# The neighbours' first layer as four column tiles, and a fp32 second layer with zero-padded weights

## The reference

```python
h = maximum(layernorm(x), 0)                          # 4096 x 256
neib_att = tanh(neigh @ Wn1 + bn1) @ Wn2 + bn2        # 4096x256 @ 256x32, then @ 32x32
value    = neigh @ Wv + bv                            # 4096 x 128
x_att    = tanh(h @ Wx1 + bx1) @ Wx2 + bx2            # 4096 x 32
ws  = leaky_relu(x_att @ neib_att.T, 0.01)            # 4096 x 4096
ws  = softmax(where(adj > 0, ws, -9e15), axis=1)
out = x + concatenate([h @ Wfx + bfx, ws @ value], axis=1)
```

## Time and profile before

| | us |
|---|---|
| median of 3 runs (519.1 to 520.16) | 519.95 |
| the profiled execution | 519.84 |
| its span, first to last instruction | 518.0 |

### The profile page before, as it was taken

One profiled execution on the slowest core, in us unless ns is written; L12 is line 12 of the kernel. 1 busy time (PEld: TensorE's weight loads), 2 busy tenths in 40 slices (PEclk: granted clock), 3 DMA queues, 4 the chain that ended last, 5 costly groups with the idle time before them and its releaser, 6 DMA issues.

```text
span 518.0 us, 8865 instructions
## 1 busy us (share of the span) xinstructions
PE 480.9 (93%) x2812; PEld 374.6 (72%) x2855; DVE 451.8 (87%) x883; ACT 417.6 (81%) x585; POOL 210.0 (41%) x324
## 2 busy tenths in 40 slices
PE   5697978799999999999999999999999999998996
PEld 4365667587778778777878777877777787766884
DVE  1679878989999899989998999899999989985664
ACT  2562797899889988998889888988899889997552
POOL 1503113145644564446544664366336444530100
PEclk9997998999999999999999999999999999999999
DMA  6864774565456544664567445744565555500100
GB/s 180 217 203 79 142 137 79 113 112 94 81 92 139 116 76 85 127 144 81 82 127 156 77 75 105 159 80 80 110 135 82 82 95 118 90 5 1 42 0 22
DMA packets 38530, 52.07 MB, mean 101 GB/s; under 512 B 4436, under 2 KB 30292, under 8 KB 38484
## 3 DMA queue, kind: packets, MB, share of 16 engines
q0 software_dynamic: 9216, 33.56, 39.3%
q1 hardware_dynamic: 29268, 17.95, 11.7%
HBM read 80.86 MB, written 4.19 MB: 164 GB/s over the span
## 4 chain that ended last, share of the span: by engine, by line
PE 55%; ACT 17%; issue 9%; POOL 7%; DVE 7%; DMA 4%; SPq 1%; DVEq 0%; ACTq 0%; POOLq 0%
PE ps_turned L904 14%; PE ps_scores L881 9%; ACT scores L515 7%; PE ps_product L925 7%; PE ps_product L923 7%; PE ps_product L924 6%; POOL scores L409 5%; ACT scores L503 5%; ACT pt_hi L479 4%; PE ps_scores L880 4%; PE ps_product L849 3%; DMA scores<-in_L_gnn_neigh 3%; DVE mask L645 2%; DVE pt_lo L658 1%; PE ps_product L787 1%
## 5 line engine op out<-in xcount | busy, mean ns | idle before, releaser
L658 DVE TENSOR_TENSOR pt_lo<-ps_turned,pt_hi 128x512 fp32r<-128x512 f32 x256 | 173.4, 684 | 34.3 <-ACT pt_hi L479 19.1
L479 ACT ACTIVATE pt_hi<-ps_turned 128x512 fp32r<-128x512 f32 x256 | 155.4, 608 | 56.5 <-PE ps_turned L904 56.2
L409 POOL TENSOR_TENSOR scores<-scores,mask 128x512 f32<-128x512 f32 x109 | 126.7, 1162 | 176.7 <-ACT scores L503 176.6
L904 PE MATMUL ps_turned<-ident,scores 128*128 128x128 f32 x1024 | 154.7, 274 | 3.6 <-DVE pt_lo L658 3.1
L904 PEld LDWEIGHTS ps_turned<-ident,scores 128*128 128x128 f32 x1024 | 124.1, 140 | 45.5 <-DVE pt_lo L658 17.2
L503 ACT ACTIVATE scores<-ps_scores 128x1024 f32<-128x1024 f32 x128 | 132.0, 1031 | 13.3 <-PE ps_scores L881 13.3
L515 ACT ACTIVATE scores<-scores,neg_top 128x2048 f32<-128x2048 f32 x64 | 129.0, 2015 | 0.0
L676 DVE CUSTOM_DVE_ANT_0 scores<-ps_scores,scores,top 128x1024 f32<-128x1024 f32 x96 | 122.5, 1276 | 3.2 <-ACT scores L503 2.7
L923 PE MATMUL ps_product<-pt_hi,v_hi 128*128 128x512 f32 x256 | 122.0, 477 | 0.2 <-DVE pt_lo L658 0.2
L881 PE MATMUL ps_scores<-neib,xs 128*128 128x512 f32 x256 | 109.9, 507 | 6.0 <-DVE top L676 2.9
L925 PE MATMUL ps_product<-pt_lo,v_hi 128*128 128x512 f32 x256 | 101.4, 396 | 0.0
(11 more groups left out here) (75 smaller groups left out, 378.1 us busy)
## 6 DMA issues: line engine op xcount, KB each, us to landing
adj_in<-in_adj POOLq DMA_DIRECT2D x64, 512.0 KB, 5.4
scores<-in_L_gnn_neigh SPq DMA_DIRECT2D x8, 512.0 KB, 5.5
x_rows<-in_x SPq DMA_DIRECT2D x8, 512.0 KB, 5.4
x_left<-in_x SPq DMA_DIRECT2D x8, 256.0 KB, 3.0
x_right<-in_x SPq DMA_DIRECT2D x8, 256.0 KB, 2.8
out_h<-x_left SPq DMA_DIRECT2D x8, 256.0 KB, 4.2
out_h<-x_right SPq DMA_DIRECT2D x8, 256.0 KB, 3.4
scores<-in_x SPq DMA_DIRECT2D x1, 512.0 KB, 4.0
```

The lines of the kernel that those rows point to most:

```text
L409: pool.tensor_tensor(half, half, mask[:, s % MASK_RING, BANK:CHUNK], ALU.add).then_inc(masked, 1)
L479: act.activation(pt_hi[:, (2 * b + u) % HI_RING], pt[:, u], ACT.Copy).then_inc(hi_done, 1)
L658: dve.tensor_tensor(pt_lo[:, u], pt[:, u], pt_hi[:, (2 * b + u) % HI_RING].bitcast(FP32), ALU.subtract).then_inc(lo_done, 1)
L904: last = pe.transpose(pt[:, u, i * P:(i + 1) * P], scores[:, parity * TILES + i, n * P:(n + 1) * P], ident[:, :])
```

## The change

The first layer of the neighbours takes the form of x's: `w1_n` is held once, 32 wide, and `first_layer` issues for each half of the contraction four matmuls of 128 neighbours each, each into its own 32 partitions of `ps_hidden`, now 128x128. Tanh is taken once in 128x128 (L444's line). The second layer is four fp32 matmuls of 128 columns, each with `w2_n[:, i, :]`, which is zero but in the 32 rows of strip i. So `hidden_stack`, `w2_stack`, the fp32r copy, the subtraction and the three DVE instructions that built `w2_stack` are gone, and with them the semaphores `hidden_hi`, `hidden_lo`, `w2_hi` and `w2_done`. `att_high` moves from DVE to ACT as an `Identity` activation with bias; in the loop it follows the tanh, for group 7 it stands in step 0. SP issues one DMA for `Wn1` where there were two, and four for `Wn2` where there was one, after a wait until POOL has zeroed `w2_n` and `w2_x`; PE and ACT still wait for all of these before turn 0 (`CONSTS_IN`).

```diff
--- before.py
+++ after.py
@@ -54,7 +54,7 @@
 DMA_RING = 512
-CONSTS_IN = 16 * 4, 16 * 6
+CONSTS_IN = 16 * 6, 16 * 6
 B2_IN = 16 * 2
@@ -140,21 +140,18 @@
         rows = scratch(4, 0, 2, TILES, D_IN)
-        hidden = scratch(4, 2048, 2, GROUP)
-        w1_n = scratch(4, 3072, KT, P)
-        w2_n = scratch(4, 3328, D_HID)
+        hidden = scratch(4, 2048, 2, P)
+        w1_n = scratch(4, 3072, KT, D_HID)
+        w2_n = scratch(4, 3328, TILES, P)
         x_ahead = scratch(5, 3072, TILES, D_IN)
         w_v = scratch(5, 0, KT, D_OUT)
-
-        hidden_stack = pt_hi[:, 0:2, :]
-        w2_stack = pt_lo[:, 0, 0:P]
 
...
         pa = ctx.enter_context(nc.psum_tensor("ps_product", [P, 2, BANK], FP32))
-        ps_hidden, ps_value = pa[:, 0, :], pt
+        ps_hidden, ps_value = pa[:, 0, 0:P], pt
         ps_att = [ps[:, 1, BANK:CHUNK], pa[:, 1, :]]
@@ -259,20 +254,19 @@
             load_neigh(0)
-            for k in range(KT):
-                sp.dma_start(w1_n[:, k].rearrange("p (r h) -> p r h", h=D_HID),
-                             wn1[k * P:(k + 1) * P, :].rearrange("p (r h) -> p r h", r=1).to_broadcast(
-                                 [P, P // D_HID, D_HID])).then_inc(consts_in[0], 16)
+            sp.dma_start(w1_n, wn1.rearrange("(k p) h -> p k h", p=P)).then_inc(consts_in[0], 16)
             sp.dma_start(b1[:, 0:1], bn1.rearrange("(r p a) -> r p a", r=1, a=1).to_broadcast(
...
             load_x_rows(0)
-            sp.dma_start(w2_n, wn2.rearrange("(r p) h -> r p h", r=1).to_broadcast(
-                [P // D_HID, D_HID, D_HID])).then_inc(consts_in[0], 16)
+            sp.wait_ge(cleared, 2)
+            for j in range(TILES):
+                sp.dma_start(w2_n[j * D_HID:(j + 1) * D_HID, j, :].rearrange("p (r h) -> p r h", h=D_HID),
+                             wn2.rearrange("p (a h) -> p a h", a=1).to_broadcast(
+                                 [D_HID, P // D_HID, D_HID])).then_inc(consts_in[0], 16)
             sp.dma_start(w1_x[:, :, :], wx1.rearrange("(k p) h -> p k h", p=P)).then_inc(consts_in[1], 16)
...
                 [P // D_HID, D_HID, 1])).then_inc(consts_in[1], 16)
-            sp.wait_ge(cleared, 1)
             for j in range(TILES):
@@ -336,6 +330,7 @@
 
+            pool.memset(w2_n, 0.0).then_inc(cleared, 1)
             pool.memset(w2_x[:, :, :], 0.0).then_inc(cleared, 1)
@@ -426,6 +421,13 @@
         def _(act):
+            def att_high(par, q):
+                if q == 0:
+                    act.wait_ge(b2_in, B2_IN)
+                act.wait_ge(second_done, q + 1)
+                act.activation(neib[:, q * GROUP:(q + 1) * GROUP], ps_att[par], ACT.Identity,
+                               bias=b2[:, 0:1]).then_inc(att_hi, 1)
+
             def turned_copy(q):
@@ -440,11 +442,10 @@
                 act.wait_ge(first_done, q + 1)
-                wait(act, hidden_lo, q - 1)
+                wait(act, second_done, q - 1)
                 act.activation(hidden[:, par], ps_hidden, ACT.Tanh, bias=b1[:, 0:1]).then_inc(hidden_done, 1)
-                act.wait_ge(hidden_done, q + 1)
-                wait(act, second_done, q - 1)
-                act.activation(hidden_stack[:, par], hidden[:, par], ACT.Copy).then_inc(hidden_hi, 1)
+                if e > 0:
+                    att_high(1 - par, q - 1)
                 if e == 1:
@@ -516,6 +515,8 @@
             def side(s):
+                if s == 0:
+                    att_high(1, NEIGH_GROUPS - 1)
                 if value_due(s - 1) is not None:
@@ -582,13 +578,7 @@
                         mask_of(n)
-                first = e == 0
-                if not first:
-                    att_high(1 - par, q - 1)
-                dve.wait_ge(hidden_hi, q + 1)
-                low = hidden_stack[P // 2:P, par]
-                dve.tensor_tensor(low, hidden[P // 2:P, par], low.bitcast(FP32), ALU.subtract).then_inc(hidden_lo, 1)
-                if not first:
+                if e > 0:
                     att_low(1 - par, q - 1)
@@ -769,10 +747,23 @@
 
+            def first_layer(q):
+                pe.wait_ge(turned_out, KT * (q + 1))
+                wait(pe, hidden_done, q)
+                for k in range(KT):
+                    for i in range(TILES):
+                        last = pe.matmul(ps_hidden[i * D_HID:(i + 1) * D_HID, :], w1_n[:, k, :],
+                                         rows_t[:, q, k * GROUP + i * P:k * GROUP + (i + 1) * P],
+                                         start=k == 0, stop=k == KT - 1)
+                last.then_inc(first_done, 1)
+
             def second_layer(par, q):
-                pe.wait_ge(hidden_lo, q + 1)
+                pe.wait_ge(hidden_done, q + 1)
                 wait(pe, att_out, q - 1)
-                pe.matmul(ps_att[par], w2_stack, hidden_stack[:, par], start=True, stop=True).then_inc(second_done, 1)
+                for i in range(TILES):
+                    last = pe.matmul(ps_att[par][:, i * P:(i + 1) * P], w2_n[:, i, :], hidden[:, par],
+                                     start=True, stop=True)
+                last.then_inc(second_done, 1)
 
@@ -781,15 +772,7 @@
                     turn_rows(q + 1, e + 1)
-                pe.wait_ge(turned_out, KT * (q + 1))
-                wait(pe, hidden_done, q)
-                for k in range(KT):
-                    last = pe.matmul(ps_hidden, w1_n[:, k, :],
-                                     rows_t[:, bass.ds(q, 1), k * GROUP:(k + 1) * GROUP].rearrange("p a n -> p (a n)"),
-                                     start=k == 0, stop=k == KT - 1)
-                last.then_inc(first_done, 1)
-                if e == 1:
-                    pe.wait_ge(w2_done, 1)
+                first_layer(q)
                 if e > 0:
```

More of the change, by code:

```diff
@@ L169, in build @@
         hidden_done = sem("hidden_done")
-        hidden_hi, hidden_lo = sem("hidden_hi"), sem("hidden_lo")
-        w2_hi, w2_done = sem("w2_hi"), sem("w2_done")
         wide_done = sem("wide_done")
@@ L474, in hi @@
                 act.wait_ge(block_turned, j + 1)
-                if b == 0:
-                    act.wait_ge(second_done, NEIGH_GROUPS)
                 if 2 * b + u >= HI_RING:
@@ L557, in x_aggr @@
                 last.then_inc(aggr_done, 1)
[L559 to L562, removed]
             def att_low(par, q):
@@ L623, in _ @@
             x_aggr(0)
[L624 to L632, removed]
             for i in range(TILES):
@@ L653, in lo @@
                 dve.wait_ge(hi_done, j + 1)
-                if b == 0:
-                    dve.wait_ge(second_done, NEIGH_GROUPS)
                 if 2 * b + u >= 2:
@@ L693, in neigh_rest @@
                 if s == 1:
-                    att_high(1, NEIGH_GROUPS - 1)
                     att_low(1, NEIGH_GROUPS - 1)
```

## The result

| | before | after |
|---|---|---|
| median, us | 520.02 (12 runs) | 516.8 (12 runs) |
| ratio to before, without the two executions named below | | 0.9939, interval 0.9919 to 0.9959 |
| the profiled execution, and its span | 519.84, 518.0 | 519.23, 517.2 |

Two of the twelve executions after took 1204 and 1842 us and are left out of the ratio; the other ten lie between 514.9 and 519.2 with a median of 516.2. So the change takes 3.2 us away by the ratio and 3.8 by the medians without those two, and the ratio's interval stays clear of 1; 514.7 was forecast. Two things must be kept apart from here on: the typical gain of 3.2 to 3.8, and the gain of 0.6 in the one execution that the profiler caught, which is the slowest of the ten. The trace can explain only the latter.

The account below looks back on a forecast made before the run. PE bounds the steady stage; its start follows an opening bound by DMA loads, then PE, then VectorE. VectorE's earlier end -5.5 and loads +0.3 give -5.2 from 519.84: 514.6, forecast 514.7 as median, range 512.9 to 517.5.

Parts of the forecast that it names:

- turns of 2.3: PE loop in the opening: after 26 us group starts lie 2.3 us apart, 2.33 computed against 2.83 before.
- Steady stage untouched, the gain kept: After the opening: no edit touches the 400 us steady stage, so its length stays and only its start moves.
- The rival in which part is given back: Between 50 and 100 us late adjacency or x's rows lose about half the gain: 517.3 us, chance 0.12.
- First layer 0.57: PE loop: the neighbours' first layer in narrow strips takes 0.57 us a group instead of 1.72.
- Second layer 0.89: PE loop: four 128-column fp32 matmuls take 0.89 us a group instead of 0.23, adding 0.66.
- Start of the loop +0.3: Opening loads up to 26.3 us: changed DMA issues and PE's clock cost +0.3 us, bounds -0.8 and +1.5.
- The clock rival: PE idles longer before 26.3 us and one group runs at half rate, costing 2.33: 517.0 us, chance 0.10.
- Tail 9.0 from `xs`: VectorE's end of the opening: `xs` high at 38.7 us, last `att_low` ending at 47.7 instead of 53.20.
- Around the span 1.8: Outside the traced span: the profiled execution's 519.84 us taken as span 518.0 and 1.8 around it.
- The loads pace the loop: Opening loop: group 6's load lands too late for the faster loop, which loses 2.0: 516.7 us, chance 0.17.
- Slower through the clock: PE stays at the low clock through the loop; four more half-rate groups cost 9.3: 524 us, chance 0.04.
- The change moves nothing: Opening loads: group 4's landing slips by 5 us and cancels the gain: 519.8 us, chance 0.03.

Follow-up runs that it names:

- after again: The kernel after, unedited, measured and traced a second time: 515.92 us, ratio 0.9931.
- idle matmuls: Kernel after plus PE matmuls whose result nobody reads, before group 0's first layer, group 2's and 4's transposes and score 0: 515.82 us, ratio 0.995.
- `att_high` on DVE: Kernel after with the bias add moved back from ScalarE to VectorE in both places: 517.6 us, ratio 0.9961.
- adjacency late: Kernel after with GpSimd's first two adjacency loads held until group 4's transposes are done: 520.73 us, ratio 1.002.
- group 2 early: Kernel after with SP issuing neighbour group 2 right behind the `Wn2` parts, ahead of the other constants: 517.98 us, ratio 0.995.
- before score 0 only: Kernel after with 8 PE matmuls whose result nobody reads, placed only ahead of score 0: 517.0 us, ratio 0.9939.
- before with the bias on ACT: Kernel before with only the bias add moved from VectorE to ScalarE: 518.65 us, ratio 0.9967.
- split: Kernel after, first adjacency load held until group 2's transposes, second until group 6's, plus 8 unread PE matmuls before score 0: 518.29 us, ratio 0.9953.
- split with more idle matmuls: Kernel after with the edits of split and 6 more unread PE matmuls ahead of group 2's transposes: 515.85 us, ratio 0.9921.
- adjacency last: Kernel after with GpSimd's first two adjacency loads held until group 6's transposes are done: 517.1 us, ratio 0.9934.

## Why the prediction was right, and where its sizes were not

The mechanism and the range were right: a shorter turn on PE and two adds fewer on VectorE in the tail bring the steady stage forward, and it keeps what it is given. The size was 1.5 to 2 us too favourable. Of the signs that the prediction named, the first layer, the bias add (0.70 on ACT) and the steady stage came true; turns of 2.3 (they are 2.53), an end of the opening near 48 (52.46) and a full clock in the wide layer did not, and in "after again" turn 4 came at 28.58, behind the 27.5 named as a sign of being wrong. There is luck in the range: it holds the median, while both traced executions of the unedited kernel (519.23 and 520.83) lie outside it.

Two slips of the prediction change nothing: the fewer pieces give back up to 1 of 0.7 to 1.3, so group 2 could come 0.3 earlier and not 0.5; and from +0.3 the bound -0.8 lies 1.1 away, and it is with 1.1 that one comes to the stated 512.9, though the text says 0.8.

For the profiled execution the sum can be closed, term by term (predicted 514.6, measured 519.23):

- *Steady stage untouched, the gain kept.* Right: span minus opening end went from 464.80 to 464.74. The rival in which part is given back has nothing to stand on.
- *First layer 0.57.* Right, in every full-rate turn.
- *Second layer 0.89.* Too small; this is the term that was mis-sized in every trace. It takes 1.09. The 0.89 of the earlier trace rows was read behind another layer of full width; here it stands behind the narrow first layer, and leaving the narrow strips costs 0.20. x's second layer, behind a wide one, still takes 0.89 (chain of the kernel with idle matmuls):

```profile
36.68 1.09 PE ps_product L768 x8
37.77 0.89 PE ps_scores L829 x8
38.67 0.57 PE ps_product L759 x16
```

  The sentence that the trace left no more than 0.13 us for the switch was wrong: it counted the way in and not the way out. The transposes behind x's narrow layer show the way out as 1.02 instead of 0.87 in the chain above, and they already did in the trace before, chain of waits:

```profile
26.33 1.09 PE ps_turned L768 x8
...
35.60 1.02 PE ps_turned L768 x8
```

  Both switches together are 0.33 a group. Up to `xs` the way out costs 0.20 in three turns, 0.15 behind x's narrow layer and 0.05 in the last turn, where the sum had the full 1.05: 0.8 us. The rule of the Trainium skill (TensorEngine Tiling (Array Packing), Tiling Modes: changing the mode drains the array) was the warning to follow, and this trace agrees; its size is read from the operation behind the switch.
- *Start of the loop +0.3.* It was +1.09. SP issued group 2 at 11.42, as before: the four `Wn2` issues took 1.93 where one took 0.57, one issue of `Wn1` less gave 0.54 back, and the next two issues took 0.8 less than before; why they did is not shown. The low clock at turn 2 (1.97 instead of 1.10) delayed group 4 by 0.93, which was named as the lever and not taken as the likely case. With the loads left as they are, turn 4 varies from 26.43 to 28.58 in other traces (`att_high` on DVE, after again).
- *The clock rival*, 0.10: it did happen in the profiled execution. Turn 4 at 4.10 and the next transposes at 1.08 are 1.57 + 0.21 = 1.8 us over the sum. Of this 0.2 is not the clock: transposes that follow a wait take 1.09 at the full clock too (26.33 above), and the sum had 0.87.
- *Tail 9.0 from `xs`.* 8.75 at the full clock, in six traces; 10.08 here, because the clock fell after 2.15 us of idling before score 0. The prediction had 1.9 of idling and no fall; after 1.60 (adjacency late) and 1.85 (group 2 early) the first scores and the wide layer did run at full rate. VectorE waited 0.95 for the wide layer, and the first masks took 0.3 longer.
- *Around the span 1.8.* Now 2.0, in this and in every variant of the kernel after (1.97 to 2.20 in the profiled executions), while the variants of the kernel before stay at 1.8. That 0.2 was in no term, and no run tells where it comes from.

Sum: 0.8 (start) + 0.8 (switch) + 1.8 (low clock and wait in the loop) + 1.1 (tail) + 0.2 (around) = 4.7, and 519.23 - 514.6 = 4.6.

For the typical execution, 516.2, only the 0.8 of the switch and the 0.2 around the span are sure; they give 515.6. The 0.6 left may be a later start of the loop or a low stretch in some of the executions. No trace shows a typical execution, and the idle matmuls, which remove the stretch in their trace, leave the median where it was, so this stays open.

*The loads pace the loop*, 0.17: did not happen in the kernel after. It did as soon as the loop started earlier: with idle matmuls group 7 made PE wait 0.30, with group 2 early group 5 made it wait 5.26. *Slower through the clock*, 0.04: from turn 4 on the clock came back within little more than a turn every time. *The change moves nothing*, 0.03: group 4 landed 1.1 later, not 5.

## What to carry to other kernels

Price an operation from a row whose neighbours are the ones it will have: the switch into narrow column tiles was in its own row, the switch out of them in the next operation's. When an opening is fed by one set of DMA engines, moving a transfer moves the wait to whoever is behind it; four other orders of the same loads were tried and none was clearly better. And one profiled execution may stand 3 to 5 us from its kernel's median: compare executions before explaining a trace.

## What the runs showed of the hardware

- Four 32-wide strips run fully beside each other (0.44 us for 16 records of 128 columns, where eight in a row take 0.87), plus 0.13 on entering and 0.15 to 0.20 on leaving.
- A wait of 2.0 to 2.7 us for one of the groups 4 to 6 was followed by a fall of the granted clock in four traces (after, after again, before score 0 only, before with the bias on ACT) and by none in three (before, 2.71 us; split, 2.21; split with more idle matmuls, 1.98). These are different edits; no single program was traced with both outcomes. What the rows show is that this one wait, by its length, does not decide it: 2.21 kept the clock and 2.09 did not.
- A neighbour load of 512 KB landed 3.2 us after its issue at best. Group 4, issued behind two adjacency loads, took 6.5 to 8.7 (nine traces), and group 5 took 9.4 in the run with group 2 early. An adjacency load took 10.6 beside x's loads (adjacency last).
